# Four chained cross-attention layers: the additive mask of the wide layers written into the score bank by ScalarE instead of by a matmul per tile

## What is computed

```python
# kind A
q, k, v = x @ Wq, ctx @ Wk, ctx @ Wv                 # 16 heads of 64
logits = einsum('bhqd,bhkd->bhqk', q, k) * 64 ** -0.5
col_bias = zeros((512, 77))
col_bias = col_bias.at[:, token_indices_A].set((-20.0 * (1.0 - mask_A))[:, None])
col_bias = col_bias.at[:, token_indices_B].set((-20.0 * (1.0 - mask_B))[:, None])
probs = softmax(logits + col_bias[None, None])
x = einsum('bhqk,bhkd->bhqd', probs, v) @ Wo + bo + x
# kind B: the same without col_bias and bo, heads of 32, q = rmsnorm(x, norm_w) @ wq
```

## Time and profile before

| | |
|---|---|
| median of 3 runs | 2314.44 us (2314.19 to 2314.68) |
| the profiled execution, its own time | 2315.51 us |
| its span, first to last instruction | 2313.4 us |
| PE busy | 2200.5 us (95%) |
| DVE, ACT, POOL busy | 58%, 36%, 26% |
| mean granted clock of PE | 0.984 |

### The profile page before, as it was taken

One profiled execution on the slowest core, in us unless ns is written; L12 is line 12 of the kernel. 1 busy time (PEld: TensorE's weight loads), 2 busy tenths in 40 slices (PEclk: granted clock), 3 DMA queues, 4 the chain that ended last, 5 costly groups with the idle time before them and its releaser, 6 DMA issues.

```text
span 2313.4 us, 31485 instructions
## 1 busy us (share of the span) xinstructions
PE 2200.5 (95%) x12120; PEld 1882.3 (81%) x12120; DVE 1338.2 (58%) x2340; ACT 835.0 (36%) x1494; POOL 600.5 (26%) x390
## 2 busy tenths in 40 slices
PE   7999899999999988899999999999999979999998
PEld 7999888888888876677778888888888857777777
DVE  5333375466555644777677656455655455677775
ACT  3222242233222423554544333222332333554443
POOL 0000041222111323443433322111211342443331
PEclk9999999999999998999999999999999989999999
DMA  7777632212221222232233322221122212233222
GB/s 206 165 165 165 153 96 70 64 41 65 64 72 46 57 72 67 75 96 76 80 86 81 92 75 63 63 72 51 52 67 66 72 37 67 70 86 80 75 60 70
DMA packets 251566, 189.73 MB, mean 82 GB/s; under 512 B 186678, under 2 KB 189142, under 8 KB 248858
## 3 DMA queue, kind: packets, MB, share of 16 engines
q1 hardware_dynamic: 251418, 187.74, 30.4%
HBM read 131.39 MB, written 56.26 MB: 81 GB/s over the span
## 4 chain that ended last, share of the span: by engine, by line
PE 65%; DVE 11%; POOL 5%; issue 4%; ACT 3%; POOLq 0%; DVEq 0%; ACTq 0%
PE acc_bank L204 7%; PE acc_bank L206 7%; PE acc_bank L205 7%; PE q_bank L746 7%; PE q_bank L750 6%; PE q_bank L748 6%; PE t_bank L761 5%; PE acc_bank L777 4%; PE acc_bank L779 4%; PE acc_bank L781 4%; DVE pT_s L997 3%; DVE sums L1009 2%; DVE prob L983 2%; POOL prob L1108 2%; DVE mx L979 2%
## 5 line engine op out<-in xcount | busy, mean ns | idle before, releaser
L1108 POOL TENSOR_TENSOR prob<-prob,rinv 128x1232 f32<-128x1232 f32 x128 | 288.2, 2252 | 718.6 <-DVE rinv L1012 718.6
L979 DVE TENSOR_REDUCE mx<-s_bank 128x4 f32<-128x308 f32 x512 | 240.0, 469 | 239.3 <-PE s_bank L714 234.1
L903 ACT ACTIVATE q_s<-q_bank 128x512 fp32r<-128x512 f32 x192 | 114.5, 596 | 700.5 <-PE q_bank L750 698.9
L997 DVE TENSOR_TENSOR pT_s<-t_bank,pT_s 103x512 fp32r<-103x512 f32 (+1 forms) x384 | 253.2, 675 | 165.1 <-ACT pT_s L909 164.4
L746 PE MATMUL q_bank<-x_s,w_s 128*128 128x512 f32 x768 | 321.5, 419 | 23.3 <-POOL w_s L1101 15.8
L204 PE MATMUL acc_bank<-o_s,w_s 128*128 128x512 f32 x768 | 314.2, 409 | 25.8 <-DVE o_s L1003 25.8
L750 PE MATMUL q_bank<-x_s,w_s 128*128 128x512 f32 x768 | 315.5, 411 | 0.0
L748 PE MATMUL q_bank<-x_s,w_s 128*128 128x512 f32 x768 | 315.1, 410 | 0.0
L206 PE MATMUL acc_bank<-o_s,w_s 128*128 128x512 f32 x768 | 306.2, 399 | 0.0
L205 PE MATMUL acc_bank<-o_s,w_s 128*128 128x512 f32 x768 | 305.8, 398 | 0.0
L1083 POOL TENSOR_TENSOR x_s<-x_front,x_s 128x512 fp32r<-128x512 f32 x124 | 159.1, 1288 | 547.3 <-ACT x_s L870 547.3
(11 more groups left out here) (91 smaller groups left out, 4213.3 us busy)
## 6 DMA issues: line engine op xcount, KB each, us to landing
stream<-x_back SPq DMA_DIRECT2D x128, 256.0 KB, 2.5
x_front<-stream SPq DMA_DIRECT2D x96, 256.0 KB, 3.5
x_back<-stream SPq DMA_DIRECT2D x96, 256.0 KB, 3.7
kvw_raw<-kvw SPq DMA_DIRECT2D x17, 1024.0 KB, 8.5
k_scr<-k_out SPq DMA_DIRECT2D x36, 308.0 KB, 8.3
keys_s<-k_scr SPq DMA_DIRECT2D x128, 77.0 KB, 2.4
v_scr<-v_out SPq DMA_DIRECT2D x8, 1024.0 KB
x_back<-x_in SPq DMA_DIRECT2D x32, 256.0 KB, 5.6
```

The source lines that it names most:

```text
L979: dve.tensor_reduce(top, scored, AX_X, ALU.max).then_inc(s_max, 1)
L997: dve.tensor_tensor(pT_s[0:rows, n, 1], t_bank[(3 * u + n) % 2][0:rows, :], pT_s[0:rows, n, 0].bitcast(F32), ALU.subtract).then_inc(t_lo, 1)
L1108: pool.tensor_tensor(view, view, rinv[:, slot].unsqueeze(2).broadcast_to([P, TILES * GH, CTX]), ALU.mult).then_inc(p_norm, 1)
```

## The change

The mask matmul goes. In its place a table `bias_s` (128 tokens x 4 tiles x 77 columns for each of layers 0 and 2) is made once by DVE in `context_block`, and ACT copies it, repeated over four heads, into the score bank before the tile's score matmuls, which now accumulate onto it (`start=False` throughout). Two matmuls at the start of `attention_block` open the two banks once. PE waits for `s_biased` where it waited for `s_sub`; ACT waits for `s_sub` before it writes. ACT's copies for tiles 0 and 1 of unit s+1 stand at the end of step s, behind `exps(s, 1)`; those for tiles 2 and 3 stand behind the first and the second query copy of step s. `beside` now has six score matmuls to place instead of seven. In the setup, four mask DMAs become one, the wait of SP for POOL's clearing goes, and the chain on DVE loses and gains some instructions.

```diff
+    def biased(self, u, t):
+        return TILES * (u - UNITS * (u // (2 * UNITS))) + t + 1
...
-        self.mask_s = sb("mask_s", [P, TOK], F32R)
-        self.hit_s = sb("hit_s", [P, PAIRS, SC], F32R)
+        self.bias_s = sb("bias_s", [P, PAIRS, TILES, CTX], F32)
...
-            sp.wait_ge(cleared, 1)
-            sp.dma_start(mask_raw[0:1], masks[0:1]).then_inc(setup_loaded, 16)
-            sp.dma_start(mask_raw[32:33], masks[0:1]).then_inc(setup_loaded, 16)
-            sp.dma_start(mask_raw[64:65], masks[1:2]).then_inc(setup_loaded, 16)
-            sp.dma_start(mask_raw[96:97], masks[1:2]).then_inc(setup_loaded, 16)
+            sp.dma_start(mask_b[:, :, :], masks).then_inc(setup_loaded, 16)
...
-            link(dve.memset(hit_s[:, :, :].bitcast(F32), 0.0))
             dve.wait_ge(consts, 5)
-            dve.wait_ge(setup_loaded, 16 * 7)
-
-            link(dve.tensor_scalar(mask_b, mask_raw, 1.0, SUPPRESS * float(KIND_A.DH) ** 0.5, ALU.subtract, ALU.mult))
-            link(dve.tensor_copy(mask_s[:, :], mask_b))
-            for row in (32, 96):
-                link(dve.tensor_tensor(mask_s[row:row + 1, :], mask_b[row:row + 1], mask_s[row:row + 1, :].bitcast(F32),
-                                       ALU.subtract))
-
+            dve.wait_ge(setup_loaded, 16 * 4)
+
+            link(dve.tensor_scalar(mask_b[:, :, :], mask_b[:, :, :], 1.0, SUPPRESS * float(KIND_A.DH) ** 0.5, ALU.subtract,
+                                   ALU.mult))
...
-                for row in (0, 32, 64, 96):
-                    link(dve.tensor_copy(hit_s[row:row + 1, p].rearrange("q (h n) -> q h n", h=GH),
-                                         cmp_t[row // 64][row:row + 1].unsqueeze(1).broadcast_to([1, GH, CTX])))
+                for t in range(TILES):
+                    link(dve.tensor_scalar(bias_s[:, p, t], cmp_t[0], mask_b[:, 0, t:t + 1], None, ALU.mult))
+                    link(dve.scalar_tensor_tensor(out=bias_s[:, p, t], in0=cmp_t[1], scalar=mask_b[:, 1, t:t + 1],
+                                                  in1=bias_s[:, p, t], op0=ALU.mult, op1=ALU.add))
...
-                after(pe, s_sub, TILES * u + t - 1)
                 if kind(u).name == "A":
-                    pe.matmul(out[:, 0:SC], mask_s[:, tok], hit_s[:, u // (2 * UNITS)], start=True, stop=False)
-                    yield
+                    pe.wait_ge(s_biased, plan.biased(u, t))
...
-                for i in range(7):
+                for i in range(6):
                     next(small, None)
-                    run(large, n * (i + 1) // 7 - n * i // 7)
-
+                    run(large, n * (i + 1) // 6 - n * i // 6)
+
+            for i in range(2):
+                mm = pe.matmul(s_bank[i][:, 0:SC], x_s[:, 0, 0, 0, 0:P], x_s[:, 0, 0, 0, 0:SC], start=True, stop=True)
+                mm.then_inc(s_opened, 1)
...
+            def bias(u, t):
+                if u >= NU or kind(u).name == "B":
+                    return
+                if u == 0 and t < 2:
+                    act.wait_ge(s_opened, t + 1)
+                after(act, s_sub, TILES * u + t - 1)
+                act.activation(s_bank[t % 2][:, 0:SC].rearrange("q (h n) -> q h n", h=GH),
+                               bias_s[:, u // (2 * UNITS), t].unsqueeze(1).broadcast_to([P, GH, CTX]), ACT.Copy)\
+                    .then_inc(s_biased, 1)
...
                 if s < NU and kind(s).name == "A":
                     next(q, None)
+                    bias(s, 2)
                     next(q, None)
+                    bias(s, 3)
                     fresh_x()
                     exps(s, 0)
...
                     turned(1)
                     turned(2)
                     exps(s, 1)
+                    bias(s + 1, 0)
+                    bias(s + 1, 1)
...
                     turned(1)
                     turned(2)
+                    bias(s + 1, 0)
+                    bias(s + 1, 1)
```

More of the change, by code:

```diff
@@ L206, in three_passes @@
     return pe.matmul(out, weights[1], moving[0], start=False, stop=stop)
-def wait_apart(eng, semaphore, value, seen):
-    eng.wait_ge(semaphore, value)
-    eng.sem_inc(seen, 1)
 class Lasting:
@@ L256, in context_block @@
         w_A, x_s, ident, mean_w, mhalf = lasting.w_s, lasting.x_s, lasting.ident, lasting.mean_w, lasting.mhalf
-        mask_s, hit_s, bo, nw = lasting.mask_s, lasting.hit_s, lasting.bo, lasting.nw
+        bias_s, bo, nw = lasting.bias_s, lasting.bo, lasting.nw
         w_s = w_A[:, 2:4]
@@ L260, in context_block @@
         tok_f = sb("tok_f", [P, 2, 8], F32)
-        mask_raw, mask_b = ctx_raw[:, 0, 0:TOK], ctx_raw[:, 1, 0:TOK]
+        mask_b = sb("mask_b", [P, 2, TILES], F32)
         iota_t = ctx_raw[:, 2, 0:CTX]
@@ L578, in attention_block @@
         s_mm, s_max, s_sub = map(sem, ("s_mm", "s_max", "s_sub"))
+        s_opened, s_biased = sem("s_opened"), sem("s_biased")
         p_exp, p_sum, p_inv, p_norm = map(sem, ("p_exp", "p_sum", "p_inv", "p_norm"))
@@ L709, in scores @@
                         cols = out[:, 2 * CTX * c:2 * CTX * (c + 1)]
-                        pe.matmul(cols, q_s[:, slot, 0, c, tok], keys[:, c, 0], start=False, stop=False)
+                        pe.matmul(cols, q_s[:, slot, 0, c, tok], keys[:, c, 0], start=False, stop=False,
+                                  skip_group_check=True)
                         yield
-                        pe.matmul(cols, q_s[:, slot, 0, c, tok], keys[:, c, 1], start=False, stop=False)
+                        pe.matmul(cols, q_s[:, slot, 0, c, tok], keys[:, c, 1], start=False, stop=False,
+                                  skip_group_check=True)
                         yield
-                        mm = pe.matmul(cols, q_s[:, slot, 1, c, tok], keys[:, c, 0], start=False, stop=c == 1)
+                        mm = pe.matmul(cols, q_s[:, slot, 1, c, tok], keys[:, c, 0], start=False, stop=c == 1,
+                                       skip_group_check=True)
                         if c == 1:
@@ L718, in scores @@
                 else:
+                    pe.wait_ge(s_sub, TILES * u + t - 1)
                     if t == 0:
@@ L924, in split_weights @@
                 act.activation(w_s[:, part, 0, QUARTER * c:QUARTER * (c + 1)], stage[:, n % 2], ACT.Copy).then_inc(w_hi, 1)
+            bias(0, 0)
+            bias(0, 1)
             for _ in split_q(0):
@@ L1151, in build @@
     boA, normB = dram("boA", (P, PAIRS, XC)), dram("normB", (P, PAIRS, XC))
-    masks, tokens = dram("masks", (2, TOK)), dram("tokens", (1, 8 * words), I32)
+    masks, tokens = dram("masks", (P, 2, TILES)), dram("tokens", (1, 8 * words), I32)
     stream = dram("stream", (B, P, XC, TOK), kind="ExternalOutput")
@@ L1208 @@
         "normB": two("norm_w", BB).reshape(PAIRS, XC, P).transpose(2, 0, 1),
-        "masks": np.stack([arr("mask_S_fk1"), arr("mask_S_fk0")]),
+        "masks": np.stack([arr("mask_S_fk1"), arr("mask_S_fk0")]).reshape(2, TILES, P).transpose(2, 0, 1),
         "tokens": np.ascontiguousarray(tokens).view(np.int32).reshape(1, -1),
```

## The result

| | before | after |
|---|---|---|
| median of the runs | 2314.41 us | 2397.76 us (2395.64 to 2399.02) |
| span of the profiled execution | 2313.4 us | 2396.9 us |
| granted clock, mean | 0.984 | 0.970 |
| PE busy | 2200.5 us (95%) | 2208.5 us (92%) |
| ACT busy | 835.0 us | 926.4 us |

The ratio is 1.0359 [1.0341, 1.0377]: slower, as forecast, and inside the range of 2346 to 2400, but 38 us above the predicted 2360. The time is rival 1's (2393): the pause came, and the clock fell behind about every second one.

The account below looks back on a forecast made before the run. PE was taken to bound the wide layers. From 2315.51: -42.3 mask matmuls, +91.4 waits for ACT's copy, -3.9 setup, +0.5 opening matmuls gave 2361.2; less 1.1 for the median, 2360 us; range 2346 to 2400.

Parts of the forecast that it names:

- rival 1: Wide layers: the clock falls behind every second new PE pause, 33 us on top, 2393 us; chance 0.33.
- Sum: -42.3 us: Wide layers: PE time saved by dropping 256 mask matmuls; bounds -36 and -59.
- the 0.23 and 0.18 us for tiles 0 and 3: PE, behind transposes: saving per mask matmul, 0.23 for tile 0 at 44 boundaries, 0.18 for tile 3.
- 44 x 2.05 = 90.2: Uncovered unit boundaries of wide layers: PE waits 2.05 us for ACT's copy into bank 0 at each of 44.
- +91.4: PE's waits for bank 0 copies at 44 boundaries plus 1.2 us at layer 2's entry; bounds +82 and +100.
- The other copies cost nothing: Wide layers: ACT's copies for tiles 1, 2 and 3 come before PE needs them and cost no time.
- -3.9 us: Setup: DVE's 2.55 us DMA wait goes, PE idles less, a lowered clock may go; bounds 0 and -5.5.
- 0 of 12: Earlier PE pauses followed by dense running: none of 12 lowered the clock; the new pause was put in this kind.
- could not happen: By the Trainium skill's rule on PSUM copies, the clock falling behind the new pause was said to be impossible.
- Rival 2: Unit boundaries: the copy ends before PE needs bank 0, the stall is hidden, 2269 us; chance 0.04.
- Rival 3: Even trade: mask matmuls worth their recorded 340 ns, 87 us, which the stall eats; 2315 us; chance 0.03.

Follow-up runs that it names:

- e3: The changed kernel with neither mask matmul nor ACT copy, the first score matmul starting the sum; 2280.89 us, ratio 0.9858.
- e9: e1 with ACT's work on fresh x moved to the step's end only where the next layer is narrow; 2276.7 us, ratio 0.9837.
- e4: The changed kernel with eight unread 512-column matmuls filling PE's pause at the 44 boundaries; 2363.55 us, ratio 1.0215.
- e1: The changed kernel with ACT's copy for tile 0 moved into the gap before ACT's tail; 2283.77 us, ratio 0.9874.
- e6: e1 with ACT's work on fresh x moved behind the tail in every wide step; 2292.54 us, ratio 0.9907.
- e7: e1 with SP's wait for POOL's clearing put back before the setup DMAs; 2282.86 us, ratio 0.9864.
- e2: The changed kernel with ACT's copy for tile 0 one place earlier, directly before the second exponentials; 2339.08 us, ratio 1.0116.
- e10: e1 unchanged, run again on the same chip as e9; 2281.76 us, ratio 0.9864.
- e5: The changed kernel with an extra 512-column ACT copy before tile 0's copy at the 44 boundaries; 2436.97 us, ratio 1.0532.
- e8: The changed kernel with four unread 512-column matmuls in PE's pause at the 44 boundaries; 2362.77 us, ratio 1.0213.

## Why the prediction was right in sign and 38 us short

**The direction and its mechanism** held: PE at its limit in the wide layers, the copy fifth in ACT's ordered tail, 44 boundaries that nothing covers.

**"Sum: -42.3 us"** for the mask matmuls was too large: 35.0. The failing step is the 0.23 and 0.18 us for tiles 0 and 3. I had written that the next matmul may inherit the 0.09 and then took half of it, or all; e3 shows that it inherits it. The lower bound, 256 x 0.14 = 36, was the truth. That is +7.3 us.

**What stands at the layer's end** was not in the sum. e3 with its -33.5 against before lacks 4.9 us of 35.0 and 3.4 for setup and openers. They are lost where the wide layers end: there PE's idle time grew from 1.94 to 2.50 us, and the clock fell behind it. With that wait removed, in e9, the kernel comes out 36.7 us below the one before measured beside it. A stretch where PE is not the bound does not give the gain back one for one.

**"44 x 2.05 = 90.2", "+91.4"**: 1.97 us by the batches of e4, and with the entries to the layers, 79.3 us shown plus 44 x (1.97 - 1.71) = 91 us in all. This term was right to 1 us, and its parts too (copy at 2.25 for 2.26, duration 437 ns for 0.45).

**"The other copies cost nothing"**: right to 3 us (e1 against e3). Inside a layer they cost nothing: the batches of e1 and e3 are alike to 0.01 us. What there is arises at the entry to layer 0, where PE waits 0.41 us for a copy, and at the layer changes, 1.01 us three times. A second wait at that entry, of 0.84 us, is not theirs: e3, which has no copies, waits as long there, for DVE's subtraction. The clock fell behind these entry waits in e1, e6, e7 and e9, and not in e2, e3 and e10.

**"-3.9 us"** for the setup: PE's idle time for the drains fell from 4.25 to 1.08 us, the low stretch behind it is gone, and the attention block began 3.7 us earlier (270.46 for 274.13). With the openers in, its first query matmul starts 3.0 us earlier (271.11), where 3.4 was predicted. I had given two reasons, SP's wait and three DMAs less; e7 shows that the wait carries only a small part.

**Rival 1** is what decided. It was priced rightly, 22 stretches at 1.5 us: there were 22, at 1.57, 34.5 us, and e4, which has none of them, is 34.2 us faster than after. It was placed second by a wrong step: I sorted the idle times of the trace into single and broken pauses and read 0 of 12 as evidence for the first kind. Ten of those twelve were 1.48 us long, shorter than the new pause, and two were 1.9 us. A class made after the fact, with two cases of the right length, could not carry a chance of 0.57 against 0.33. The very pause that stood for the safe kind is 2.5 us long in e1, e3, e7 and e10, and there the clock fell with six of eight; where it is 2.3 us long, in after, e2, e4, e5 and e8, with four of ten. I had noted that the new pause was longer and came 44 times, and gave that too little weight. The Trainium skill ("TensorE: Matmul & The Clock Gate", Loop structure matters more than you think) had it that a copy out of PSUM between tiles doesn't break the warmth; but its sketch lets the next tile's matmuls follow immediately, and the prediction's "could not happen" left that condition out. The runs show the case that it leaves out: here the next matmul waits for a copy into its bank, and the clock fell with 22 of 42 such waits.

The sum again, from what the runs showed: 2280.9 (e3) + 91 for the pauses + the low clock. e3 has its own low stretches, at the layers' ends; up to 2010 us of each trace I count 75.0 us at half clock in e3 and 129.6 in after, 16 stretches of 3.4 us more, 25 us. Together 2397; measured 2397.8.

**Rival 2** named its own cure: the copy overtakes the exponentials. As forecast for this kernel it was rightly given little; as an edit it is e1. **Rival 3** is excluded by the 0.137 us per matmul.

## What to carry to other kernels

An operation that moves from the bound engine to an idle one costs what its place in that engine's ordered list makes of it: look for the idle time just ahead of the engine's tail, not at its mean load, and put the work there before anything else is judged. Price a stall on the bound engine twice, by its length and by the clock behind it, and take the nearest idle times by their length; two of them are no evidence. Where a stall comes back in a fixed rhythm, the falls of the clock can too: a share counted in one kernel is that kernel's. A gain on the bound engine ends where something else is the bound: list the places (here the layer's end) where it already waits for another.

## What the runs showed of the hardware

Of pauses of PE every 14 to 16 us between dense work, a fall of the granted clock to 0.50 went with 20 of 40 when they were 1.71 us long, with 31 of 40 at 2.23 us, and with none of 40 at 1.11 us and at 0.79 us. In layer 0 of the changed kernel the falls came back every 160 us, two batches, at the same places. A low stretch lasted 3.4 us and cost 1.57 us. Eight matmuls without a use, in a stall that was there anyway, made the kernel 34 us faster, and four did the same.
